# A graph network on one core: own h as a count on the diagonal, attribute sums turned once

## The reference

```python
src, dst = edge_index[0], edge_index[1]
for l in range(3):
    msg = h[src] + h_edge_attr
    agg = segment_sum(msg, dst, num_segments=n)
    out = agg + h
    z = gelu(layernorm(out @ W1[l].T + b1[l], g1[l], be1[l]))
    z = layernorm(z @ W2[l].T + b2[l], g2[l], be2[l])
    h = gelu(z + h)
```

## Time and profile before

| | us |
|---|---|
| median of 3 runs (4749.45 to 4756.9) | 4749.83 |
| the profiled execution | 4744.73 |
| its span, first to last instruction | 4742.9 |
| PE busy in the span (87%) | 4128.7 |
| VectorE busy (62%) | 2953.9 |
| GpSimd busy (42%) | 1971.8 |
| ScalarE busy (41%) | 1934.4 |

### The profile page before, as it was taken

The page is one execution under the profiler, slowest core; times in us unless marked ns, Lnnn a source line. Parts: engine busy times, 40 slices in busy tenths (PEclk is TensorE's granted clock), DMA queues, the critical chain, the costliest instruction groups (busy, mean ns, idle before and its releaser), DMA issues.

```text
span 4742.9 us, 100574 instructions
## 1 busy us (share of the span) xinstructions
PE 4128.7 (87%) x35231; PEld 3732.7 (79%) x35231; DVE 2953.9 (62%) x8147; ACT 1934.4 (41%) x4188; POOL 1971.8 (42%) x2199
## 2 busy tenths in 40 slices
PE   1499999999976788888898888888888999999997
PEld 1499999999975577787787787787888777777876
DVE  7799999999943344444444444444444667777777
ACT  1566666666641222222222222222213666666664
POOL 5511111111127777777777777777772000000000
PEclk9799999999998899999999999999999999999999
DMA  5444444444455566777676766766778787887885
GB/s 121 170 204 208 208 205 203 203 203 203 203 181 138 143 201 199 206 207 204 203 208 200 210 204 200 204 201 203 212 203 251 227 240 210 245 238 215 262 251 165
DMA packets 793921, 967.67 MB, mean 204 GB/s; under 512 B 124439, under 2 KB 674055, under 8 KB 781143
## 3 DMA queue, kind: packets, MB, share of 16 engines
q1 hardware_dynamic: 623488, 764.12, 47.9%
q0 software_dynamic: 60048, 125.37, 10.6%
q10 hardware_dynamic: 110151, 75.61, 6.2%
HBM read 707.25 MB, written 257.60 MB: 203 GB/s over the span
## 4 chain that ended last, share of the span: by engine, by line
PE 40%; POOL 34%; issue 14%; DVE 8%; DMA 3%; ACT 1%; POOLq 0%; ACTq 0%; DVEq 0%
POOL ACC L1048 33%; PE ps L1581 9%; PE ps L1950 8%; PE ps L1951 8%; PE ps L1565 4%; PE ps L1567 4%; DMA ACC<-table,BIG 2%; DVE T L2227 2%; DVE BIG L2227 2%; PE ps L1866 1%; POOL ACC L972 1%; PE ps L1968 1%; PE ps L1986 1%; PE ps L1955 1%; DVE COUNTS L2543 1%
## 5 line engine op out<-in xcount | busy, mean ns | idle before, releaser
L1048 POOL DMA_INDIRECT ACC<-table,BIG x1715 | 1681.6, 981 | 626.1 <-issue 511.1
L1851 PE MATMUL ps<-BIG 128*128 128x257 f32 x3430 | 859.0, 393 | 138.5 <-ACT BIG L1249 137.9
L2470 DVE TENSOR_TENSOR BIG<-ps,ACC 128x512 f32<-128x512 f32 (+1 forms) x441 | 297.9, 675 | 1076.6 <-DMA ACC<-table,BIG 848.2
L1851 PEld LDWEIGHTS ps<-BIG 128*128 128x128 f32 x3430 | 633.7, 195 | 238.2 <-ACT BIG L1249 158.0
L1249 ACT ACTIVATE BIG<-BIG 128x512 f32<-128x512 f32 (+1 forms) x441 | 273.7, 621 | 1319.7 <-DVE BIG L2470 1314.9
L1581 PE MATMUL ps<-H,ACC 128*128 128x128 f32 x4802 | 689.9, 284 | 0.0
L1382 ACT ACTIVATE COUNTS<-X 128x512 fp32r<-128x512 bf16 (+1 forms) x1092 | 600.9, 599 | 161.9 <-PE ps L1951 156.4
L1581 PEld LDWEIGHTS ps<-H,ACC 128*128 128x128 f32 x4802 | 588.0, 191 | 0.2 <-ACT ACC L1190 0.2
L1190 ACT ACTIVATE BIG<-ps 128x392 bf16<-128x392 f32 x784 | 390.3, 498 | 468.3 <-PE ps L1567 468.3
L1950 PE MATMUL ps<-COUNTS,H_BIG 128*128 128x512 f32 (+1 forms) x1274 | 510.2, 400 | 30.9 <-DVE COUNTS L2543 15.0
L1951 PE MATMUL ps<-COUNTS,H_BIG 128*128 128x512 f32 (+1 forms) x1274 | 489.3, 384 | 0.0
(11 more groups left out here) (290 smaller groups left out, 7589.0 us busy)
## 6 DMA issues: line engine op xcount, KB each, us to landing
X<-count_mat SPq DMA_DIRECT2D x360, 512.0 KB, 4.8
weight_mat<-ACC SPq DMA_DIRECT2D x49, 3136.0 KB, 9.2
BIG<-in_edge_attr SPq DMA_DIRECT2D x392, 256.0 KB
count_mat<-BIG SPq DMA_DIRECT2D x49, 1568.0 KB, 12.8
REL_WT<-weight_mat SPq DMA_DIRECT2D x275, 256.0 KB
BIG<-rel_tab ACTq DMA_DIRECT2D x392, 128.0 KB
BIG<-weight_mat SPq DMA_DIRECT2D x176, 256.0 KB
X<-count_mat SPq DMA_DIRECT2D x108, 384.0 KB, 3.7
```

The lines of the kernel that those rows point to most:

```text
L1048: pool.indirect_dma_start(GR[:, q * QUAD + u, :], None, tables[1], bass.IndirectOffsetOnAxis(ap=STEP_IDX[:, b % 3, r * QUAD + u:r * QUAD + ...
L1851: mm = pe.matmul(PS[4 + par][:, 0:HIW], DR[:, q * QUAD + u, :], HB[:, q * QUAD + u, :], start=(r == 0 and u == 0), stop=(r == QB - 1 and u ...
L2470: dve.tensor_tensor(HB[:, steps, 0:F], PS[n % 2][:, 0:size * F].rearrange("p (u f) -> p u f", f=F), GR[:, own, :], ALU.add).then_inc(rows_ ...
```

## The change

Own h becomes one more count: GpSimd adds the identity to the 128x128 part of a count block in which destinations and sources are the same nodes (`own_counts`), before SP stores the block. The attribute sums are transposed in the edge stage, by a third transpose of `turned_rows`, and lie transposed in `ATT` and `T1`. So the matmuls with the identity go, and VectorE adds T1 while it copies the product from PSUM to `SB_SUM` (`sum_turned`, in place of ScalarE's copy). The shift becomes a step of its own at 12 positions before the end of the superblock (`shifted`), and z moves from lag 5 to lag 6.

```diff
-OWN_SUMS = [40 if g == 0 else SB_END[g - 1] + 12 for g in range(SB_COUNT)]
-LAG_OF = {"sum_turned": 4, "z": 5, "z_bias": 9, ...
+LAG_OF = {"sum_turned": 4, "z": 6, "z_bias": 9, ...
+SHIFTED_AT = {e - 12: g for g, e in SB_END.items()}
...
+        ATT_B = of_acc(at + 8 * F, F)[0]
...
-        act_converted, dve_converted, counts_used, own_ready, high_ready = csum_part, osum_ready, z_std, oT_ps, rest_step
+        diag_added = y_stats
+        act_converted, dve_converted, counts_used, high_ready = csum_part, osum_ready, z_std, rest_step
...
             def store_block(b, par, i):
                 sp.wait_ge(group_out, (b + 1) * GROUPS + BANKS)
                 sp.dma_start(weight_mat[b, :, :], WB[par]).then_inc(mat_out[par], 16)
+                wait_alone(sp, diag_added, b + 1)
                 sp.dma_start(count_mat[b, :, :], CB[par]).then_inc(mat_out[par], 16)
...
                         if s == 0:
-                            sp.wait_ge(csum_ps, (LAYERS - 1) * SBS)
+                            sp.wait_ge(counts_used, SB_END[(LAYERS - 1) * SBS - 1])
...
+            def own_counts(b, par, i):
+
+                wait_alone(pool, count_out, (b + 1) * GROUPS + BANKS)
+                own = CB[par][:, bass.ds(b * P, P)]
+                pool.tensor_tensor(own, own, ident[:, :], ALU.add).then_inc(diag_added, 1)
             def staged_blocks():
-                block_pairs(pool, staged_block)
+                staged_block(0, 0, 0)
+                with pool.Fori(0, BLOCKS // 2) as i:
+                    staged_block(i * 2 + 1, 1, i)
+                    own_counts(i * 2, 0, i)
+                    staged_block(i * 2 + 2, 0, i + 1)
+                    own_counts(i * 2 + 1, 1, i)
+                own_counts(BLOCKS - 1, 0, BLOCKS // 2)
...
             def turned_rows(b):
                 act.activation(MEAN_T, PS[2][:, 0:P], ACT.Copy)
-                act.activation(OLD_T, PS[2][:, P:2 * P], ACT.Copy).then_inc(node_free, 1)
+                act.activation(OLD_T, PS[2][:, P:2 * P], ACT.Copy)
+                act.activation(ATT[:, b, 0:F], PS[2][:, 2 * P:3 * P], ACT.Copy).then_inc(node_free, 1)
...
-            def sum_turned(g): 
-                l, nb, own = of_sb(g)
-                act.wait_ge(csum_ps, g + 1)
-                act.activation(SB_SUM[:, 0:nb, :], PS[g % 2][:, 0:nb * P].rearrange("p (b d) -> p b d", d=P), ACT.Copy).then_inc(oT_sb, 1)
...
                 pe.transpose(PS[2][:, 0:P], MEAN_B, ident[:, :])
-                pe.transpose(PS[2][:, P:2 * P], OLD_B, ident[:, :]).then_inc(node_ps, 1)
+                pe.transpose(PS[2][:, P:2 * P], OLD_B, ident[:, :])
+                pe.transpose(PS[2][:, 2 * P:3 * P], ATT_B, ident[:, :]).then_inc(node_ps, 1)
...
-                pe.matmul(to, H_R[l][:, h, 1, :], counts, start=False, stop=False).then_inc(counts_used, 1)
-                if at == SB_END[g]:
-                    pe.wait_ge(own_ready, g + 1)
-                    for j in range(nb):
-                        mm = pe.matmul(PS[g % 2][:, j * P:(j + 1) * P], SB_SUM[:, j, :], ident[:, :], start=False, stop=(j == nb - 1))
-                    mm.then_inc(csum_ps, 1)
+                pe.matmul(to, H_R[l][:, h, 1, :], counts, start=False, stop=(at == SB_END[g])).then_inc(counts_used, 1)
...
             def sums_out(b):
                 dve.tensor_copy(HS[b % 3], PS[4 + b % 2][:, 0:F])
-                dve.tensor_copy(ATT[:, b, :], PS[4 + b % 2][:, F:2 * F + 1]).then_inc(block_out, 1)
+                if b:
+                    dve.wait_ge(node_free, NODE_USES["turned", b - 1])
+                dve.tensor_copy(ATT_B, PS[4 + b % 2][:, F:2 * F])
+                dve.tensor_copy(ATT[:, b, F:F + 1], PS[4 + b % 2][:, 2 * F:2 * F + 1]).then_inc(block_out, 1)
...
-            def own_sums(g):
+            def sum_turned(g):
                 l, nb, own = of_sb(g)
                 if g == 0:
                     dve.wait_ge(attr_moved, C1)
                 else:
                     dve.wait_ge(z_ps, g)
+                dve.wait_ge(counts_used, SB_END[g])
+                dve.tensor_tensor(SB_SUM[:, 0:nb, :], PS[g % 2][:, 0:nb * P].rearrange("p (b d) -> p b d", d=P), T1[:, own, :], ALU.add).then_inc(oT_sb, 1)
+
+            def shifted(g):
+                l, nb, own = of_sb(g)
                 if l:
                     dve.wait_ge(gelu_done, g - SBS + 1)
                 elif g == 0:
                     dve.wait_ge(newh, BLOCKS + C1)
-                dve.tensor_tensor(SB_SUM[:, 0:nb, :], H[:, own, :], T1[:, own, :], ALU.add).then_inc(own_ready, 1)
                 if g % SBS == 0:
                     dve.wait_ge(layer_in, LAYERS * 128 if l else 128)
                 step("shift", g, dve.tensor_tensor(H[:, own, :], H[:, own, :], over_nodes(L_BE2[l], nb), ALU.add))
...
-                    if pos in OWN_SUMS:
-                        own_sums(OWN_SUMS.index(pos))
+                    if pos in TURNED_AT:
+                        sum_turned(TURNED_AT[pos])
+                    if pos in SHIFTED_AT:
+                        shifted(SHIFTED_AT[pos])
```

More of the change, by code:

```diff
@@ L185 @@
     SB_CHAIN.append(max(SB_END[_g], SB_CHAIN[-1] + CHAIN if _g else 0))
-OWN_SUMS = [40 if g == 0 else SB_END[g - 1] + 12 for g in range(SB_COUNT)]
-LAG_OF = {"sum_turned": 4, "z": 5, "z_bias": 9, "z_stats": 11, "z_moments": 13, "z_guess": 14, "z_root1": 16, "z_root2": 18, "z_root3": 20, "z_norm": 22,
+LAG_OF = {"sum_turned": 4, "z": 6, "z_bias": 9, "z_stats": 11, "z_moments": 13, "z_guess": 14, "z_root1": 16, "z_root2": 18, "z_root3": 20, "z_norm": 22,
           "z_turned": 24, "z_gelu": 27, "y": 29, "y_bias": 33, "y_stats": 35, "y_moments": 37, "y_guess": 38, "y_root1": 39, "y_center": 40, "y_root2": 41,
@@ L1503, in dense_layers @@
                 for pos in range(LAYER_END):
-                    if pos in TURNED_AT:
-                        sum_turned(TURNED_AT[pos])
                     for g in behind(pos, "z_gelu"):
```

## The result

The changed kernel takes 4777.6 us (median of four runs, 4773.2 to 4782.9) against 4749.6 us: a ratio of 1.0061, 95% interval 1.0048 to 1.0074. It is slower by 28 us, and the forecast was 16 us faster. The profiled execution after has a span of 4776.1 us, 33.2 more than the one before.

| stretch | before | after | difference | forecast |
|---|---|---|---|---|
| start to the first gather (matrix stage) | 1385.1 | 1436.6 | +51.5 | +7 |
| first to last gather (edge stage) | 2203.3 | 2203.6 | +0.25 | 0 |
| last gather to the first item of the layers | 92.4 | 96.7 | +4.3 | +0.6 |
| first item to the end (layer stage) | 1062.0 | 1039.2 | -22.8 | -23.1 |

A forecast was written before the change was run, and what follows sets the result against it. PE was taken to bound the matrix and layer stages, GpSimd's gathers the edge stage. Matmuls -32.7, shift +16.8, z -7.2, edge +0.6 and matrix +7 gave -15.5 us: 4749.83 to 4734 us, range 4725 to 4743.

The forecast's parts named there:

- The step that failed: Matrix stage: GpSimd's next staging, moved behind the addition, is needed only one block later; given no cost.
- that rate: Matrix stage: VectorE's one-hot group loses 0.32 us per us of overlap with GpSimd, from 0.58 us for 1.80.
- A smaller misreading: Matrix stage: VectorE's first two one-hot groups are what PE waits for, so the addition costs wherever it falls in them.
- The addition: Matrix stage: GpSimd's 128x128 addition, about 0.40 us long, costs 0.15 us a block, 7 us in all; bounds 0 and 19.
- Rival 2: Matrix stage: GpSimd's addition holds the ports for 0.40 us in VectorE's second group; +19 for +7, 4746 us; chance 0.20.
- Rival 3: Matrix stage: the count store goes late and ScalarE waits for its buffer; up to 322 us, 5056 us; chance 0.08.
- The shift's term: Layer stage: H + be2 enters VectorE's gapless run, 0.60 us per four-block and 0.47 per three-block superblock; 16.8 us more.
- rival 1: Layer stage: the shift is covered and costs nothing, so 4717 us; chance 0.17.
- The sign named for it: Layer stage: PE's wait before a superblock's last item, for ScalarE, should grow from 0.69 to about 1.3 us.
- The z-run of three blocks: Layer stage: two additions leave VectorE's run before z, saving 0.80 us per three-block superblock; 7.2 us less.
- the forecast's 23.1: Layer stage as a whole, matmuls, shift and z together: 23.1 us less.
- Rival 4: Layer stage: VectorE's wait for the last item delays conversions behind it and PE waits; 4748 us, no change; chance 0.07.

The follow-up runs named there:

- wait_alone: Changed kernel with GpSimd's wait for the last count copy kept ahead of the next staging, but the addition left out; 4765.0 us, ratio 1.0040.
- staging_first: Changed kernel with one order turned round: GpSimd stages block b+2 before it adds the diagonal of block b; 4742.0 us, ratio 0.9995.
- both_hidden: Changed kernel with staging before the addition, and the addition held back until VectorE's third one-hot group is finished; 4728.4 us, ratio 0.9969.
- both_hidden_shift31: As both_hidden, with the shift H + be2 also put 31 items behind the last superblock's end; 4710.4 us, ratio 0.9932.

## Why the prediction was wrong

**The step that failed** is a sentence of the matrix stage: "GpSimd's next staging also stands behind it, and that is needed one block later." It costs a moved step at nothing because its deadline is far. But the staging had a cover that it lost: VectorE's pause, in which four of its seven instructions lay. Behind the addition it meets VectorE's second and third group. That is 0.86 of the 1.09 us a block (wait_alone), about 41 of the 51.5 us. The prediction had the price in hand: it read 0.32 us for each us of staging that overlaps VectorE's run, from 1.80 us of overlap. The staging after lies whole in the run, 1015.72 to 1020.54, 4.82 us: 3.02 more, by that rate 0.97 a block. It was applied to the addition alone. The runs show 0.86 in the place of that nothing. A smaller misreading stands beside it: the first two groups are named as those that PE waits for, where the rows show waits for the second, and after the change for the third too.

**The addition** was put at 0.15 a block (bounds 0 and 0.40) and measured 0.20 to 0.25. Its bounds held, and so did the rate; the duration was too short. Beside VectorE's run the addition took 0.69 to 0.72 us, not the estimated 0.40, and 0.32 per us of that is 0.22 to 0.23.

**Rival 2** named blocks 23.8 us apart for an addition that takes the ports; they came out 24.51. Its place was right (VectorE's groups that PE waits for), its culprit mostly wrong. **Rival 3** did not happen: in the profile after ScalarE waits only for PE. In staging_first it waited once for a stored count block, 3.6 us.

**Layers.** The shift's term was right, so rival 1 falls: cycles of four changed by 0.60 and cycles of three by 0.5, for the 0.60 and 0.47 that make up its 16.8. Between both_hidden and both_hidden_shift31 the layers differ by 18.8. About 1.7 of this is scatter: one cycle of the third layer, which took 29.7 to 32.7 us in the runs, fell by 2.3 where its neighbours fell by 0.6. The sign named for it, 1.3 us of wait before the last item, appeared as 0.78 there and 0.25 one item earlier; the cycle, 26.8 forecast and 26.7 to 26.9 measured in the first two layers, is the better sign. **The z-run of three blocks** was over-sized: 0.80 each, 7.2 in all. With no shift in the y-run that cycle of three takes 22.70 for 23.76 before, of which the matmuls are 0.67; 0.39 is left, 3.5 in all. So z to z the layers won 19.5 us, under the forecast's 23.1; the sum with 3.5 in place of 7.2 gives 19.4. That first item to end gives 22.8 is partly luck: 3.25 of it lies before the first z, a stretch that took 46.7 us before, 43.5 after and 43.5 to 46.4 in the other runs.

**Rival 4**: VectorE waits 0.35 us for the end of a superblock, but nothing behind it was late, and the cycle fell by what the rest of the sum gives.

## What to carry to other kernels

A new instruction in an engine's queue moves everything behind it. Ask of each moved step not only when it is needed, but beside what it will now run: a deadline a block away hid no cost, because the staging slowed another engine, not its own consumer. Contention was paid here only in the instructions that the bound engine waits for; the same overlap behind VectorE's third group cost nothing, since VectorE had a pause ahead. And a step whose inputs are ready early belongs into the wait before a gapless run, not into it.

## What the runs showed of the hardware

The addition is stretched in two quite different ways. In the second group (staging_first) it takes 0.72 us and VectorE loses 0.24. Behind the third group it took 2.40 us, and VectorE lost next to nothing (GpSimd and VectorE, both_hidden):

```profile
1009.16 2.40 POOL L1008 TENSOR_TENSOR BIG<-BIG,ident 128x128 f32 x1 [6.44 <-ACT BIG L1211]
...
1009.74 1.53 DVE L2238 TENSOR_TENSOR T<-T,BIG 128x800 bf16<-128x800 bf16 x3
1011.19 0.27 DVE L2216 TENSOR_TENSOR X<-X,ps 128x128 f32 x1
1011.39 0.60 DVE L2234 TENSOR_TENSOR BIG<-NODE,BIG 128x800 bf16<-128x800 bf16 x1
```

It ends at 1011.56, 0.37 us behind the start of VectorE's only instruction there with an operand in PSUM; its shortest duration anywhere is 0.43. In the first block, where VectorE has no such instruction, the addition after took longest and ended 0.28 us into VectorE's next pause (GpSimd, after):

```profile
205.74 18.13 POOL L1006 TENSOR_TENSOR BIG<-BIG,ident 128x128 f32 x1 [19.16 <-ACT BIG L1205]
```

This fits the Trainium skill (page "SBUF — State Buffer", section "Who interferes with whom"), which says that a VectorE instruction with two SBUF inputs contends with a GpSimd instruction that reads SBUF, and one with at most one SBUF input, outside the 2-port modes, does not. Why the addition gets in between two instructions of VectorE's run in one place and waits through the run in another, no run here settles; both are seen in nearly every block.
